# A two-layer graph network and a routed FFN on one core: the first layer's weight product moved behind the adjacency product

## The reference, cut to what matters

```
def gnn(x, adj, W1, b1, W3, b3, Wf, bf):          # x: 2048 x 256, adj: 2048 x 2048
    h = relu(adj @ (x @ W1) + b1)                 # layer 1
    h = relu(adj @ (h @ W3) + b3)                 # layer 2
    return tanh(h @ Wf + bf)
x = x + gnn(layernorm(x), adj, ...)
x = x + ffn(layernorm(x), ...)     # 8 experts, each token goes to 2 of them
```

## Time and profile before

| | |
|---|---|
| median of 3 runs | 711.06 us (710.85 to 712.42) |
| the profiled execution | 713.51 us |
| its span in the trace | 711.6 us |
| TensorE, VectorE, ScalarE busy, share of the span | 90%, 51%, 47% |
| layer 1, chunk 0 | 17.57 to 63.94 us |
| layer 1, products of chunks 1 to 3 | 63.94 to 159.59 us |

### The profile page before, as it was taken

The page is one execution under the profiler, slowest core; times in us unless marked ns, Lnnn a source line. Parts: engine busy times, 40 slices in busy tenths (PEclk is TensorE's granted clock), DMA queues, the critical chain, the costliest instruction groups (busy, mean ns, idle before and its releaser), DMA issues.

```text
span 711.6 us, 11911 instructions
## 1 busy us (share of the span) xinstructions
PE 642.2 (90%) x3501; PEld 541.1 (76%) x3502; DVE 363.6 (51%) x851; ACT 332.4 (47%) x658; POOL 108.9 (15%) x105
## 2 busy tenths in 40 slices
PE   1999999999999798766897799999998999999992
PEld 1988888887777677544686688888887888888882
DVE  3776444565457868486751233375665373333330
ACT  1567465775456757364541233455563353233330
POOL 3000000000000000005656521111111111111111
PEclk9999999999999999855897699999999999999996
DMA  8983000000043203402753221062565111110111
GB/s 307 343 356 119 1 0 1 24 7 0 1 140 126 89 0 133 163 31 55 274 183 90 61 30 15 10 189 72 143 183 184 15 15 15 15 15 9 14 15 17
DMA packets 32294, 61.54 MB, mean 86 GB/s; under 512 B 2978, under 2 KB 24868, under 8 KB 30212
## 3 DMA queue, kind: packets, MB, share of 16 engines
q1 hardware_dynamic: 25060, 51.13, 20.2%
q0 software_dynamic: 6912, 9.70, 7.9%
q10 hardware_dynamic: 288, 0.26, 0.1%
HBM read 52.05 MB, written 9.04 MB: 86 GB/s over the span
## 4 chain that ended last, share of the span: by engine, by line
PE 81%; DVE 7%; issue 5%; ACT 3%; DMA 2%; DVEq 0%; POOL 0%; SPq 0%; ACTq 0%; POOLq 0%
PE bank L1254 40%; PE bank L1139 8%; PE bank L1141 7%; PE bank L1140 7%; PE bank L1115 4%; PE bank L1299 4%; PE bank L1178 3%; DMA adj_s<-in_adj 2%; PE bank L1152 2%; PE bank L1103 2%; PE bank L1194 1%; PE bank L1247 1%; DVE ring L736 1%; PE bank L1176 1%; DVE ew L1025 1%
## 5 line engine op out<-in xcount | busy, mean ns | idle before, releaser
L1254 PE MATMUL bank<-ew,xeT 128*128 128x512 f32 x840 | 207.2, 404 | 4.6 <-DVE ew L1025 3.5
L1254 PEld LDWEIGHTS bank<-ew,xeT 128*128 128x128 f32 x840 | 160.2, 194 | 38.6 <-issue 5.8
L1254 PE MATMUL bank<-ew,heT 128*128 128x256 f32 x840 | 115.6, 295 | 8.5 <-issue 6.3
L736 DVE TENSOR_TENSOR ring<-adj_s,ring 128x512 fp32r<-128x512 f32 x128 | 87.8, 688 | 67.7 <-ACT adj_s L500 41.4
L1254 PEld LDWEIGHTS bank<-ew,heT 128*128 128x128 f32 x840 | 108.2, 200 | 11.0 <-issue 11.0
L1139 PE MATMUL bank<-ring,Z 128*128 128x512 f32 x256 | 110.0, 430 | 6.5 <-DVE ring L736 6.3
L1141 PE MATMUL bank<-ring,Z 128*128 128x512 f32 x256 | 100.9, 394 | 0.0
L1140 PE MATMUL bank<-ring,Z 128*128 128x512 f32 x256 | 100.3, 392 | 0.0
L436 POOL DMA_INDIRECT xg<-ffn_in_rows,idx x39 | 48.0, 1231 | 340.8 <-DVE idx L976 317.7
L640 ACT ACTIVATE sil<-bank 128x512 f32<-128x512 f32 x70 | 41.9, 599 | 123.1 <-PE bank L1254 104.2
L452 POOL DMA_INDIRECT out<-y_st,idx_st x35 | 54.6, 1561 | 250.6 <-issue 238.1
(11 more groups left out here) (161 smaller groups left out, 659.0 us busy)
## 6 DMA issues: line engine op xcount, KB each, us to landing
w_raw<-in_L_ffn_W SPq DMA_DIRECT2D x24, 1024.0 KB, 5.5
adj_s<-in_adj SPq DMA_DIRECT2D x16, 1024.0 KB, 6.1
x_in<-in_x SPq DMA_DIRECT2D x4, 512.0 KB, 4.9
x_res<-in_x SPq DMA_DIRECT2D x4, 512.0 KB, 3.5
out<-x SPq DMA_DIRECT2D x4, 512.0 KB, 2.9
ffn_in_rows<-x_res SPq DMA_DIRECT2D x4, 512.0 KB, 2.9
xg<-ffn_in_rows,idx POOLq DMA_INDIRECT x39
out<-y_st,idx_st POOLq DMA_INDIRECT x35, 3.8
```

Of the source, the lines that this page charges most:

```text
L736: nc.vector.tensor_tensor(lo, src, hi, ALU.subtract).then_inc(s_lo, 1)
L1254: last = nc.tensor.matmul(out_ap, stat[:, sl, k, :], w_at(k, wl), start=(k == k0 and sl == wl == 0), stop=(k == k1 - 1 and sl == 1))
```

## The change

Layer 1 is computed as (adj @ norm(x)) @ W1 instead of adj @ (norm(x) @ W1). `Z` now holds the split of norm(x) itself: no transposes of x, no product by W1 in chunk 0; ScalarE and VectorE split four tiles at a time with one instruction each (`x_hi`, and part 3 of `x_norm`).

The product by W1 comes behind each chunk instead, as `h_rows(c)`: 12 matmuls with 512 columns, behind `product` 3 of the next chunk. It needs the accumulators split first: `a_hi` on ScalarE (two copies, behind block 2), `a_lo` on VectorE (two subtractions, behind block 3). The rest of the chain is moved back: `hidden1` to blocks 6 and 7, `h_lo` to block 8, `z2_rows` to products 7 and 8, `z2_out` to blocks 10 and 11. For the last four tiles (in layer 2) `z_hi` and `z_lo` read PSUM directly and `z2_out` falls away. The buffers of W1's split and of `aT` take other places in memory; `aT` shares its place with `hTs`. The last two loads of `adj` wait for the split of x instead of the products by W1.

```
@@ -57,9 +57,9 @@
...
         Z = at("Z", [P, 2, NT, D], F32R, 128)
-        z2 = at("z2", [P, NT, D], F32, 160)
-        W1s = at("W1s", [P, 2, KD, D], F32R, 160)
-        xTs = at("xTs", [P, 2, 2, KD, P], F32R, 168)
+        z2 = at("z2", [P, NT - CT, D], F32, 160)
+        W1s = at("W1s", [P, 2, KD, D], F32R, 172)
+        aT = at("aT", [P, 2, KD, CW], F32R, 176)
         x_res = at("x_res", [P, CT, D], F32, 160)
...
@@ -351,7 +352,7 @@
...
                 if t == NT - 2:
-                    sp.wait_ge(s_zp, NT)
+                    sp.wait_ge(s_zlo, NT)
                 sp.dma_start(adj_s[:, t, :], adj_rows[t, :, :]).then_inc(s_adj[t % 2], 16)
...
@@ -474,17 +475,10 @@
...
 
-            def x_T(t):
-
-                act.wait_ge(s_xtp, t + 1)
-                if t >= 2:
-                    act.wait_ge(s_zp, t - 1)
-                nc.scalar.copy(xTs[:, t % 2, 0, :, :], x_p[t % 2][:, 0:D].rearrange("p (k n) -> p k n", k=KD)
-                               ).then_inc(s_xt, 1)
-
-            def z1_hi(t):
-                act.wait_ge(s_zp, t + 1)
-                nc.scalar.copy(Z[:, 0, t, :], sm[t % 2][:, 0:D]).then_inc(s_zhi, 1)
+            def x_hi(g):
+
+                act.wait_ge(s_xn, g + 1)
+                nc.scalar.copy(Z[:, 0, CT * g:CT * (g + 1), :], x_in[:, CT * g:CT * (g + 1), :]).then_inc(s_zhi, CT)
 
...
@@ -509,8 +503,13 @@
...
                     act.wait_ge(s_z2p, CT * c)
+                nc.scalar.copy(aT[:, 0, f, :], acc[c % 2][f][:, :]).then_inc(s_a, 1)
+
+            def hidden1(c, f):
+
+                act.wait_ge(s_hp, KD * (c + 1))
                 for out_f in (hTs[:, 0, f, :], hTf[:, 1, f, :]):
-                    last = nc.scalar.activation(out_f, acc[c % 2][f][:, :], ACT.Relu, bias=bT[:, 0, f:f + 1])
+                    last = nc.scalar.activation(out_f, sm[f][:, :], ACT.Relu, bias=bT[:, 0, f:f + 1])
                 last.then_inc(s_h1, 1)
...
@@ -527,6 +526,11 @@
...
 
+                if t >= NT - CT:
+                    act.wait_ge(s_z2p, t + 1)
+                    act.wait_ge(s_mm, S1)
+                    nc.scalar.copy(Z[:, 0, t, :], sm[t % 2][:, 0:D]).then_inc(s_zhi, 1)
+                    return
                 act.wait_ge(s_z2, t + 1)
...
@@ -577,22 +579,24 @@
...
                     roots(2 + s // CT)
+                if s < NT - CT and s % CT == 2:
+                    x_hi(1 + s // CT)
                 if s == CT:
...
                         act.dma_start(rows[N:N + P, :], zero_rows[:, :]).then_inc(s_zero, 16)
-                if s < NT - 1:
-                    if s < NT - 2:
-                        x_T(s + 2)
-                    z1_hi(s + 1)
-                if NT <= s < S1 + NT and jb in (1, 2):
-                    hidden1(s // NT - 1, jb - 1)
+                if NT <= s < S1 + NT and jb == 2:
+                    a_hi(s // NT - 1, 0)
+                    a_hi(s // NT - 1, 1)
+                if NT <= s < S1 + NT and jb in (6, 7):
+                    hidden1(s // NT - 1, jb - 6)
                 if jb == 1 and s > S1 + NT:
...
                     z_hi(jb - 2)
-                if layer == 1 and c == 0 and 7 <= jb < 7 + CT:
-                    z_hi(NT - CT + jb - 7)
+                if layer == 1 and c == 0 and jb in (10, 11):
+                    z_hi(NT - CT + 2 * jb - 20)
+                    z_hi(NT - CT + 2 * jb - 19)
                 if layer == 1 and c >= 2:
...
@@ -712,17 +716,11 @@
...
                     last.then_inc(s_xn, 1)
-
-            def x_T_lo(t):
-
-                dve.wait_ge(s_xt, t + 1)
-                nc.vector.tensor_tensor(xTs[:, t % 2, 1, :, :], x_p[t % 2][:, 0:D].rearrange("p (k n) -> p k n", k=KD),
-                                        xTs[:, t % 2, 0, :, :].bitcast(F32), ALU.subtract).then_inc(s_xtlo, 1)
-
-            def z1_lo(t):
-                dve.wait_ge(s_zhi, t + 1)
-                nc.vector.tensor_tensor(Z[:, 1, t, :], sm[t % 2][:, 0:D], Z[:, 0, t, :].bitcast(F32),
-                                        ALU.subtract).then_inc(s_zlo, 1)
+                if part == 3:
+                    dve.wait_ge(s_zhi, CT * (g + 1))
+                    tiles = slice(CT * g, CT * (g + 1))
+                    nc.vector.tensor_tensor(Z[:, 1, tiles, :], x_in[:, tiles, :], Z[:, 0, tiles, :].bitcast(F32),
+                                            ALU.subtract).then_inc(s_zlo, CT)
 
...
@@ -737,8 +735,15 @@
...
                 dve.wait_ge(s_zhi, NT + t + 1)
-                nc.vector.tensor_tensor(Z[:, 1, t, :], z2[:, t, :], Z[:, 0, t, :].bitcast(F32),
+                src = sm[t % 2][:, 0:D] if t >= NT - CT else z2[:, t, :]
+                nc.vector.tensor_tensor(Z[:, 1, t, :], src, Z[:, 0, t, :].bitcast(F32),
                                         ALU.subtract).then_inc(s_zlo, 1)
+
+            def a_lo(c, f):
+
+                dve.wait_ge(s_a, KD * c + f + 1)
+                nc.vector.tensor_tensor(aT[:, 1, f, :], acc[c % 2][f][:, :], aT[:, 0, f, :].bitcast(F32),
+                                        ALU.subtract).then_inc(s_alo, 1)
 
...
@@ -922,21 +927,14 @@
...
                                             ALU.subtract).then_inc(s_w1s, 1)
-            x_T_lo(0)
-            x_T_lo(1)
             x_norm(1, 0)
-            z1_lo(0)
             for s in range(2 * S1):
...
                 lo_of_block(s)
-                if s < NT - CT - 1 and (s + 1) % CT < 3:
+                if s < NT - CT - 1:
                     x_norm(1 + (s + 1) // CT, (s + 1) % CT)
-                if s < NT - 2:
-                    x_T_lo(s + 2)
-                if s < NT - 1:
-                    z1_lo(s + 1)
                 if s == NT - 5:
...
@@ -947,14 +945,18 @@
...
                     if jb == 3:
+                        a_lo(before, 0)
+                        a_lo(before, 1)
+                    if jb == 8:
                         h_lo(before)
-                    if jb in (5, 6):
-                        z2_out(CT * before + 2 * jb - 10)
-                        z2_out(CT * before + 2 * jb - 9)
+                    if jb in (10, 11):
+                        for t in (CT * before + 2 * jb - 20, CT * before + 2 * jb - 19):
+                            if t < NT - CT:
+                                z2_out(t)
+                            else:
+                                z_lo(t)
                 if layer == 0 and c == NC - 1 and 2 <= jb < NT - CT + 2:
                     z_lo(jb - 2)
-                if layer == 1 and c == 0 and 7 <= jb < 7 + CT:
-                    z_lo(NT - CT + jb - 7)
                 if layer == 1 and c >= 2:
...
@@ -1082,28 +1084,6 @@
-            def x_T(t):
-            def z1_rows(t):
...
@@ -1120,17 +1100,17 @@
...
                 pe.wait_ge(s_lo, s + 1)
-                if n == 0:
-                    pe.wait_ge(s_zlo, jb + 1)
+                if n == 0 and jb % CT == 0:
+                    pe.wait_ge(s_zlo, jb + CT)
                 if n == NC:
...
                     if n - 2 < NC:
-                        pe.wait_ge(s_h1, KD * (n - 1))
+                        pe.wait_ge(s_alo, KD * (n - 1))
                     else:
...
                     if n >= NC + 2:
-                        pe.wait_ge(s_xt, NT + CT * (n - NC - 1))
+                        pe.wait_ge(s_xt, CT * (n - NC - 1))
                 hi, lo = ring[:, s % RING, 0, :], ring[:, s % RING, 1, :]
...
@@ -1141,11 +1121,26 @@
...
 
+            def h_rows(c):
+
+                pe.wait_ge(s_w1s, 1)
+                pe.wait_ge(s_alo, KD * (c + 1))
+                if c >= 1:
+                    pe.wait_ge(s_z2, CT * c)
+                for f in range(KD):
+                    for k in range(KD):
+                        for al, wl in ((0, 0), (0, 1), (1, 0)):
+                            last = nc.tensor.matmul(sm[f][:, :], W1s[:, wl, k, f * P:(f + 1) * P], aT[:, al, k, :],
+                                                    start=(k == al == wl == 0), stop=(k == KD - 1 and al == 1))
+                    last.then_inc(s_hp, 1)
+
             def z2_rows(t):
...
                 pe.wait_ge(s_hlo, c + 1)
-                if t >= 2:
+                if t >= NT - CT + 2:
+                    pe.wait_ge(s_zlo, NT + t - 1)
+                elif t >= 2:
                     pe.wait_ge(s_z2, t - 1)
...
@@ -1203,25 +1198,20 @@
...
 
-            for t in range(2):
-                x_T(t)
-            z1_rows(0)
             transpose_block(0)
...
                     pe.wait_ge(s_w, 7 * 16)
-                if s < NT - 1:
-                    if s < NT - 2:
-                        x_T(s + 2)
-                    z1_rows(s + 1)
                 if s + 2 < S1:
...
                 product(s)
-                if NT <= s < S1 + NT and jb in (4, 5):
-                    z2_rows(CT * (s // NT - 1) + 2 * jb - 8)
-                    z2_rows(CT * (s // NT - 1) + 2 * jb - 7)
+                if NT <= s < S1 + NT and jb == 3:
+                    h_rows(s // NT - 1)
+                if NT <= s < S1 + NT and jb in (7, 8):
```

(43 more changed lines are left out.)

## The result

The changed kernel is slower: 714.13 us (median of 11 runs, 710.78 to 716.71) against 708.46 us for the kernel before in 11 runs (707.35 to 712.42). The ratio is 1.0056, with a 95% interval of 1.0037 to 1.0075, so +4.0 us (2.6 to 5.3). The two medians by themselves lie 5.7 us apart; this text goes by the ratio and its interval. Forecast were +4.0 and 715.0. The forecast started from the first three runs of the kernel before (median 711.06); the other eight took 707.35 to 710.80 us. The profiled executions alone would mislead: 712.89 us after and 713.51 before.

What follows compares the result with a forecast made beforehand. Up to the end of layer 1 the time was taken as the sum of TensorE's work. The terms -12.7 + 11.2 + 5.45 + 0 gave +4.0 us on the median 711.06, so 715.0 us, range 711.9 to 718.9.

Steps and rivals of the forecast that it cites:

- Chunk 0, -12.7: Chunk 0 without x's transposes and the product by W1 ends at about 51.2 us, 12.7 us earlier.
- The bound by TensorE alone: Chunk 0 if only TensorE's work counted: fifteen steps of 1.83 us, ending at 50.2, 13.7 us earlier.
- the walk: Chunk 0's schedule stepped through, each piece when engine and input are ready: product 3 at 27.05, 7.7 us per group.
- The product by W1, 11.2: Behind each chunk: twelve matmuls at 0.23 us add 2.8 us, 11.2 us in four chunks, with nothing hiding them.
- First wait 0.55, second 1.05: Each chunk's moved chain: TensorE waits 0.55 us for `h_lo` before `z2_rows`, 1.05 us for `z2_out` before the third tile.
- A: Start of the transposes in step 4 of a chunk, just behind the product by W1; `product` 7 ends at A+7.33.
- Chunk 3, 2.25: In chunk 3 ScalarE's extra `z_hi` per block makes the wait before `z2_rows` 1.2 us, the chunk's waits 2.25 us.
- Layer 2's start, 0: At layer 2's start, 0.4 us of new wait set off against 1.3 us of old waits as 0, bounds -1.3 and +1.2.
- Rival 1: TensorE's sum decides alone: no new waits, chunk 0 gives 13.7 us, so faster, 708.6 us; chance 7%.
- Rival 2: Chunk waits half as long, 0.8 to 1 us a chunk, chunk 0 gives 13.5: no change, 711.6 us; chance 15%.
- Rival 3: TensorE's clock falls in the new gaps of three chunks, +6.8 us on top, 721.8 us; chance 3%.
- Rival 4: Chunk 0 becomes VectorE's, giving 10.4 instead of 12.7, and waits 1 us longer in sum: 718.4 us; chance 15%.

## Why the prediction was right

The sign, the two waits and the price of the product came out as forecast. That the ratio gives exactly the +4.0 of the sum is in part luck: its interval is 2.6 to 5.3, and from product 0 to 127 the trace has +5.9 us, of which an earlier product 0, one draw, took back 1.0. By its steps:

- **Chunk 0, -12.7.** Measured -11.8. The bound by TensorE alone was named as 13.7, and VectorE's handovers as what takes some of it; the loss to them was put too low. The slow start lasted to about 22.9 instead of 22.1, so the first product reached its successor at 23.57, but by product 3 little of that was left (27.22 against the 27.05 of the walk). The first full group then took 8.25 us (27.22 to 35.47) instead of 7.7, the second 7.84 (35.47 to 43.31). In the first group VectorE's split of x started 0.53 us after the copy it waits for had ended, where 0.10 is usual, and that is most of the 0.55 us. It repeats in all six kernels with the split behind block 2, in this group alone, and in none of the three with the split later; its cause stays open. Moving the split by one block, with the same work, took nearly the whole loss away, which shows that it was the handovers.
- **The product by W1, 11.2.** Shown: doubled, it adds 2.8, 2.8, 2.8 and 2.7 us. From product 3 to 4 of a chunk the kernel after takes 4.56 us instead of 1.83, so a product by W1 costs 2.73 and the four 10.9. `a_hi` and `a_lo` in front of it fit, since TensorE has no idle time at L1133.
- **First wait 0.55, second 1.05.** The profile has 0.55 and 0.98 us of idle time. In TensorE's starts they cost a little more (70.23 against 69.51 and 74.71 against 73.56: 0.7 and 1.15), because a matmul usually starts 0.23 us behind one that lasts 0.39, and behind a wait that overlap of some 0.16 us is gone. `h_lo` was walked to A+7.83 and ended at A+7.89 (70.09, with A at 62.20). A chunk lost 4.65 us where 4.4 was forecast.
- **Chunk 3, 2.25.** With the product 5.05 forecast, 5.20 measured. The first wait is longer here, 1.12 us of idle time instead of 0.55:

```profile
144.44 1.67 PE L1147 MATMUL bank<-W3s,hTs 128*128 128x256 f32 x12 [1.12 <-issue]
```

That the two `z_hi` more make the difference was the forecast's reason, and the size fits (0.57 against 0.65), but no run moved them.
- **Layer 2's start, 0.** Forecast +2.8 with the product; measured +2.28. Before, the waits there make products 66 to 68 take 0.9 us more to their successors than the same products without a wait. After, product 71 starts at 174.53, its `z2_rows` could come at 175.90, and it came at 176.27:

```profile
174.95 1.22 DVE L751 TENSOR_TENSOR hTs<-hTf,hTs 128x1024 fp32r<-128x1024 f32 x1
...
176.27 1.67 PE L1147 MATMUL bank<-W3s,hTs 128*128 128x256 f32 x12 [0.21 <-issue]
```

So the old waits weighed more than the new 0.4 us: a term of -0.5, inside its bounds.
- **The sum.** At product 127 the trace has +4.96 where the steps make +4.0; chunk 0 came out 0.9 us short, the three chunks behind it together cost 0.6 more than forecast, and layer 2's start 0.5 less. Layer 2's first product, named as a sign at 1.2 us late, was 2.7 late. The ratio says +4.0 (2.6 to 5.3).

Rival 1 (no waits) is refuted by the waits themselves. Whether its direction was right is less clear: the kernel with `z2_rows` later, which has no such waits, takes 0.1 to 0.4 us less than before from product 0 to 127, and its two ratios are 0.9954 and 0.9983, the second with 1 inside its interval. With the split of x later too the kernel is faster than before (0.9963, 0.9936 to 0.9990). Rival 2 (half the waits) fell with the second one at its full size. Rival 3 fell too: the granted clock, the third value from the end, stays at 1.00 in the profile after, with waits of 0.5 and 1 us in each chunk:

```profile
53.00:159.00 106.00, 100.89 (x561) 83.77 (x561) 46.26 (x78) 61.95 (x122) 0.00 (x0) 1.00 0.06 24
```

The section cited there, "HAM oscillation — how this bites in real kernels" of the Trainium skill's "TensorE: Matmul & The Clock Gate", tells of a clock that falls while the engine waits for transfers. No run here shows that fall behind these waits for VectorE. Since the granted clock also reads 1.00 in the slow start, the pace is the better sign: behind the first wait, product 8's matmuls start at 72.41, 72.64 and 72.87 us, the usual 0.23 us apart. Rival 4 had the right mechanism for chunk 0, in a smaller size.

What I can't settle is the last 0.2 to 0.3% of any of these ratios.

## What to carry to other kernels

When engines are scheduled by hand around a pipeline with a fixed lead, each piece's place has to be checked against the places of what it waits for: a consumer one step ahead of its producer's step costs the difference in every round, however idle the producer is. Here `hidden1`, `h_lo` and `z2_out` moved five places and `z2_rows` three, and that alone cost more than the change could have brought. And a product that moves from a small operand's side to a large result's side should be priced in columns first: here eight short matmuls in each of 15 steps (14.6 us) became twelve long ones in each of four chunks (11.2 us forecast, 10.9 measured), so 3.4 to 3.7 us was all there was to gain.

## What the runs showed of the hardware

- In all these programs the stage behind layer 2 varies between executions with the share of time at the lower of TensorE's two clock levels: 417.25 us at a mean granted clock of 0.93 and 424.80 us at 0.90, for the same 2102 matmuls. Up to the end of layer 2 the mean granted clock is 1.00 in all eleven profiles.
- The slow start of TensorE differs too, though the granted clock reads 1.00 in it: from product 0 to product 1 took 2.82 us in the profile after, 2.27 with the split later, and 3.44 with `z2_rows` later, where the work is the same. I had taken its end as fixed at 22.1 us.
- The low part of x in the group that is split at 33 us started 0.53 us after ScalarE's copy had ended (33.59 against 33.06), where the others followed within 0.15 us. The five other kernels with the split behind block 2 show the same 0.54 to 0.55 us in this group. No row names a cause.
